# Nearest-code refinement with codes stored as 129-component rows

## The reference

```
x = x + L0(gn(x))   # 3x3 conv -> softmax weights for five dilated 3x3 filters; 1x1 conv; batch norm
x = x + L1(gn(x))   # for each pixel the nearest of 8192 codes (128 components)
x = x + L2(gn(x))   # depthwise 3x3 with kernels from the pooled image
x = x + L3(gn(x))   # two deformable 3x3 convs, each with group norm and relu
```

```
d   = sum(z**2) + sum(codebook**2, axis=1) - 2 * z @ codebook.T
idx = argmin(d, axis=1)
out = codebook[idx]
```

## Time and profile before

| | us |
|---|---|
| median of 3 runs | 1754.48 (1754.34 to 1756.48) |
| profiled execution | 1753.79 |
| its span | 1752.0 |
| PE busy | 1330.8 (76%) |
| DVE busy | 1173.5 (67%) |
| POOL busy | 1039.5 (59%) |
| ACT busy | 413.9 (24%) |

### The profile page before, as it was taken

How to read it: one execution, slowest core, us unless ns; L and a number is a source line. 1 busy time by engine, 2 the same in 40 slices (tenths; PEclk the granted TensorE clock), 3 DMA queues, 4 the chain that set the end, 5 groups by cost and what they waited for, 6 DMA issues and landing times.

```text
span 1752.0 us, 22932 instructions
## 1 busy us (share of the span) xinstructions
PE 1330.8 (76%) x7898; PEld 923.5 (53%) x7898; DVE 1173.5 (67%) x1526; ACT 413.9 (24%) x1280; POOL 1039.5 (59%) x950
## 2 busy tenths in 40 slices
PE   5899999398889987689645468688776877867775
PEld 2455555153344443244345456677666675766675
DVE  4578687689999999988843763654455444564444
ACT  2240000324423332242321122132211221111111
POOL 4268576205444344244477877677777777777772
PEclk9899999699999998899866778898887988878877
DMA  4020000102111111052256579678787887777773
GB/s 148 29 92 1 1 0 0 43 1 55 52 40 43 43 43 49 6 159 84 56 161 180 167 209 278 192 229 247 228 245 210 247 243 235 224 231 211 210 211 117
DMA packets 104985, 228.66 MB, mean 131 GB/s; under 512 B 16740, under 2 KB 54372, under 8 KB 104620
## 3 DMA queue, kind: packets, MB, share of 16 engines
q0 software_dynamic: 59328, 191.30, 37.5%
q1 hardware_dynamic: 45548, 35.97, 6.6%
HBM read 205.15 MB, written 22.07 MB: 130 GB/s over the span
## 4 chain that ended last, share of the span: by engine, by line
POOL 29%; PE 19%; issue 18%; DVE 12%; ACT 1%; DMA 1%; DVEq 0%; POOLq 0%; ACTq 0%
POOL code_region L1745 11%; POOL max_region L1745 6%; POOL late_region L1745 6%; POOL early_region L1745 5%; PE score L1200 4%; PE score L1201 4%; PE score L1202 4%; PE score L1221 3%; DVE max_region L1591 3%; DVE x L266 2%; DVE code_region L1626 2%; PE turn_ps L1230 1%; PE turn_ps L1100 1%; DVE fine L1456 1%; DMA late_region<-in_codes,code 1%
## 5 line engine op out<-in xcount | busy, mean ns | idle before, releaser
L1591 DVE SCALAR_TENSOR_TENSOR max_region<-score,nc,max_region 128x512 f32<-128x512 f32 x504 | 351.3, 738 | 40.1 <-PE score L1202 37.8
L1745 POOL DMA_INDIRECT code_region<-corners,lead_region x261 | 248.5, 952 | 79.5 <-issue 79.2
L1626 DVE TENSOR_TENSOR code_region<-score,code_region 128x4608 f32<-128x4608 f32 x29 | 143.6, 4956 | 137.7 <-DMA code_region<-corners,lead_region 137.4
L1221 PE MATMUL score<-ident,code_region 128*128 128x128 f32 x1044 | 153.2, 319 | 73.4 <-DVE code_region L1626 73.4
L674 POOL TENSOR_TENSOR prod_acc<-prod_acc,prod_pool 128x752 f32<-128x752 f32 (+8 forms) x112 | 149.1, 1331 | 96.2 <-DVE prod_pool L647 88.8
L1221 PEld LDWEIGHTS score<-ident,code_region 128*128 128x128 f32 x1044 | 147.5, 169 | 78.2 <-DVE code_region L1626 78.2
L1393 ACT COPY code_region<-score 128x384 f32<-128x384 f32 x144 | 68.5, 479 | 410.3 <-PE score L1221 410.3
L1745 POOL DMA_INDIRECT max_region<-corners,lead_region x126 | 125.3, 995 | 46.1 <-issue 38.1
L1745 POOL DMA_INDIRECT early_region<-corners,lead_region x135 | 127.7, 946 | 41.0 <-issue 40.8
L1745 POOL DMA_INDIRECT late_region<-corners,lead_region x126 | 127.6, 1012 | 38.9 <-issue 38.1
L1200 PE MATMUL score<-early_region,code_region 128*128 128x512 bf16 x320 | 122.5, 383 | 25.9 <-DVE max_region L1591 19.6
(11 more groups left out here) (197 smaller groups left out, 2674.9 us busy)
## 6 DMA issues: line engine op xcount, KB each, us to landing
corners<-lead_region SPq DMA_DIRECT2D x72, 192.0 KB, 4.6
corners<-lead_region SPq DMA_DIRECT2D x8, 576.0 KB, 6.8
code_region<-corners,lead_region POOLq DMA_INDIRECT x261, 3.7
codes_t<-in_codes_t SPq DMA_DIRECT2D x8, 512.0 KB, 3.7
codes_n<-in_codes SPq DMA_DIRECT2D x8, 512.0 KB, 3.5
x<-in_x SPq DMA_DIRECT2D x2, 1152.0 KB, 6.5
out<-x SPq DMA_DIRECT2D x4, 576.0 KB, 3.2
early_region<-corners,lead_region POOLq DMA_INDIRECT x135, 3.7
```

The lines of the kernel that those rows point to most:

```text
L1221: mm = pe.matmul(tps[g][:, k * P:(k + 1) * P], quads[T % SLOTS][:, 3 * g + k, c * P:(c + 1) * P], ident, start=c == 0, stop=c == CORNERS - ...
L1591: dve.scalar_tensor_tensor(r, score[SLOT[k]][:], nc2[:, m:m + 1], r, ALU.add, ALU.max).then_inc(dve_took, 1)
L1626: dve.tensor_tensor(q4, bc(wps[:, u * n:(u + 1) * n], P), q4, ALU.mult).then_inc(weighted, 1)
L1745: pool.indirect_dma_start(quads[T % SLOTS][:, k, :], None, table[j].rearrange("n s c -> n (s c)"), bass.IndirectOffsetOnAxis(index[j % B][ ...
```

## The change

The half norms are no longer a tensor of their own. `CodeNorms` becomes `CodeRows`: each slot has room for 129 components a code. A group is loaded into components 0 to 127 of its slot, ACT squares it and then writes minus half the sums into component 128, and SP stores the slot in DRAM as `code_rows`, of 1032 numbers for a block of eight codes. SP stores group g - 2 and waits until it has landed before it loads group g. `gather` reads `code_rows`; the multiply's z has a 129th component of 1, set once, so ACT's sum over 129 products is the score. On DVE `subtract` and `select` are gone, and their places in `parts`. POOL multiplies the block's number by 8 behind each gather and adds the place in `fetch`, before the fetch's DMA.

```diff
-class CodeNorms:
+class CodeRows:
...
+        self.cn = tools.sb(ctx, "codes_n", [P, self.SLOTS, PER, ROW])     # ROW = P + 1
...
     def sp(self, sp):
+        def store(g):
+            sp.wait_ge(self.appended, g + 1)
+            sp.dma_start(self.code_rows[g * P:(g + 1) * P, :], self.cn[:, g % self.SLOTS].rearrange("p j c -> p (j c)"))\
+                .then_inc(self.stored, 16)
+
         for g in range(GROUPS):
             s = g % self.SLOTS
             if g >= self.SLOTS:
-                sp.wait_ge(self.squared, PER * (g - self.SLOTS + 1))
-            sp.dma_start(self.cn[:, s, :], self.a["codes"][g * P:(g + 1) * P, :]).then_inc(self.cn_in[s], 16)
-        sp.wait_ge(self.halved, 2)
-        sp.dma_start(self.half_norms.rearrange("(g p) j -> p g j", p=P),
-                     self.c2.rearrange("p (g j) -> p g j", g=GROUPS)).then_inc(self.stored, 16)
-        sp.wait_ge(self.stored, 16)
+                store(g - self.SLOTS)
+                sp.wait_ge(self.stored, 16 * (g - self.SLOTS + 1))
+            rows = self.a["codes"][g * P:(g + 1) * P, :].rearrange("r (j c) -> r j c", c=P)
+            sp.dma_start(self.cn[:, s, :, 0:P], rows).then_inc(self.cn_in[s], 16)
+        for g in range(GROUPS - self.SLOTS, GROUPS):
+            store(g)
+        sp.wait_ge(self.stored, 16 * GROUPS)
...
     def act(self, act):                       # in the loop over g, behind the eight squares
+            act.wait_ge(self.squared, PER * (g + 1))
+            act.mul(self.cn[:, s, :, P], self.c2[:, g * PER:(g + 1) * PER], -0.5).then_inc(self.appended, 1)
...
-        act.mul(self.c2[:], self.c2[:], 0.5).then_inc(self.halved, 1)
...
-                act.copy(zt, z_ps[:]).then_inc(zt_ready, 1)
+                act.copy(zt[:, :, 0:P], z_ps[:]).then_inc(zt_ready, 1)
...
-            def subtract(n, u): ...
-            def select(n, u): ...
             def fine_find(n, u):
-                apart.wait_ge(sel_step, 1 + 4 * (PXT * (n - 1) + u) + 1)
+                apart.wait_ge(summed, PER * (PXT * (n - 1) + u + 1))
...
-                        for i, part in enumerate((subtract, fine_find, fine_place, select))}}
+                        for i, part in enumerate((fine_find, fine_place))}}
...
             def gather(n, u):
-                pool.indirect_dma_start(cand[u % 2], None, a["codes"], off).then_inc(cand_in[u % 2], 16)
-                pool.indirect_dma_start(half[:, u, :], None, half_norms, off).then_inc(cand_in[u % 2], 16)
+                pool.indirect_dma_start(cand[u % 2], None, code_rows, off).then_inc(cand_in[u % 2], 16)
+                pool.tensor_scalar(block_code[:, u:u + 1], block_id[:, u, 0:1], float(PER), None, ALU.mult)\
+                    .then_inc(block_coded, 1)
             def multiply(n, u):
-                v = cand[u % 2].rearrange("p (j c) -> p j c", c=P)
-                zb = zt[:, u, :].unsqueeze(1).to_broadcast([P, PER, P])
+                v = cand[u % 2].rearrange("p (j c) -> p j c", c=ROW)
+                zb = zt[:, u, :].unsqueeze(1).to_broadcast([P, PER, ROW])
                 pool.tensor_tensor(v, v, zb, ALU.mult).then_inc(multiplied, 1)
             def fetch(n, u):
-                apart.wait_ge(sel_step, 1 + 4 * (PXT * c + u + 1))
+                pool.wait_ge(sel_step, 2 * (PXT * c + u + 1))
+                pool.wait_ge(block_coded, PXT * c + u + 1)
+                pool.tensor_tensor(code[:, u:u + 1], block_code[:, u:u + 1], fine_id[:, u, 0:1], ALU.add)\
+                    .then_inc(coded, 1)
+                apart.wait_ge(coded, PXT * c + u + 1)
...
             pool.sem_inc(x_added, 1)
+            pool.memset(zt[:, :, P:ROW], 1.0).then_inc(ones_ready, 1)
+            pool.wait_ge(ones_ready, 1)
             pool.memset(zeros, 0.0).then_inc(zeroed, 1)
```

More of the change, by code:

```diff
@@ L40 @@
 PX = 512
+ROW = P + 1
 NPX = N // PX
@@ L704, in layer0 @@
                    (gb[:], a["gamma_beta"])])
-            ch, cl, nc2, half_norms = codes
+            ch, cl, nc2, code_rows = codes
             with ExitStack() as parts:
@@ L709, in layer0 @@
             with ExitStack() as parts:
-                beside = CodeNorms(nc, tools, parts, a, nc2, half_norms)
+                beside = CodeRows(nc, tools, parts, a, nc2, code_rows)
                 branches(nc, tools, xpad, wta, wtb, sel_a, sel_b, w_scale, y, stats, beside)
@@ L861, in carve, with finale @@
     return out
-def finale(nc, tools, a, half_norms, x, xpad, ident, gm32, gm8, nc2, depthwise, norm, places, out):
+def finale(nc, tools, a, code_rows, x, xpad, ident, gm32, gm8, nc2, depthwise, norm, places, out):
     PXT, STEPS = PX // P, GROUPS // 2
@@ L921, in finale @@
         block_id = tools.sb(ctx, "block_id", [P, PXT, 8], U32)
-        half = tools.sb(ctx, "half", [P, PXT, PER])
+        block_code = tools.sb(ctx, "block_code", [P, PXT], U32)
         fine = tools.sb(ctx, "fine", [P, PXT, PER])
@@ L1279, in sum_products @@
                 for j in range(PER):
[L1280 removed]
+                    v = cand[u % 2][:, j * ROW:(j + 1) * ROW]
                     act.activation(v, v, ACT.Identity, accum_out=fine[:, u, j:j + 1]).then_inc(summed, 1)
@@ L1450, in place_block @@
                 dve.max_index(block_id[:, u, :], best[:, u, :], maxima[(n - 1) % 2][:, u, :]).then_inc(found, 1)
[L1454 to L1456 removed]
             def fine_find(n, u):
[L1459 removed]
+                apart.wait_ge(summed, PER * (PXT * (n - 1) + u + 1))
                 dve.max(fine_best[:, u, :], fine[:, u, :]).then_inc(sel_step, 1)
             def fine_place(n, u):
[L1463 removed]
+                apart.wait_ge(sel_step, 2 * (PXT * (n - 1) + u) + 1)
                 dve.max_index(fine_id[:, u, :], fine_best[:, u, :], fine[:, u, :]).then_inc(sel_step, 1)
[L1466 to L1471 removed]
             def choose(n, u):
[L1474 removed]
                 fine_find(n, u)
                 fine_place(n, u)
[L1477 removed]
             def subtract_z(n):
```

42 lines of the change are left out of this document (15 added, 27 removed).

## The result

| | before | changed |
|---|---|---|
| median of the runs, us | 1755.48 (1753.09 to 1757.47, 6 runs) | 1743.25 (1739.09 to 1747.83, 6 runs) |
| ratio to before | | 0.9928, 95% interval 0.9908 to 0.9948 |
| the profiled execution, and its span, us | 1753.79, 1752.0 | 1742.20, 1740.4 |
| DVE busy in the stretch of the earlier trace rows, us | 488.46 | 475.46 |

The change is 12.2 us faster; 16.6 were forecast, to 1737.9. The time of 1743.25 lies in the range of 1732 to 1748, but outside the likeliest case's own range (1733 to 1741). What happened is, in the main, the forecast in the search together with a small piece of rival A' at the start.

A forecast was written before the change was run, and what follows sets the result against it. DVE was taken to bound the search, PE close behind, and POOL's row gathers the last 816 us; 10.3 + 2.8 + 1.9 + 1.6 = 16.6 us gained, 1753.79 - 16.6 + 0.69 = 1737.9 us, range 1732 to 1748.

The forecast's parts named there:

- the likeliest case: The forecast itself: gains in search and first job, no cost at the start; 1737.9 us, chance 0.56.
- rival A': First stage: store chain partly late, slot cycle 11 to 15 us, PE stands 1 to 14; 1740 to 1751, chance 0.18.
- What bounds, and the search: DVE sets the search's pace, PE close behind; without stalls chunks 1 to 5 take 51.2 us each, gaining 10.3.
- The 20.3 us of blocked DVE: Search: excess time of the two small DVE operations, L1456 and L1470, over some 0.15 us each.
- B: Search: the stall was mostly hidden by PE's backlog and waits with ACT; gain 6.5, 1748 us, chance 0.08.
- C: Search: DVE freed wholly, steps 2 and 3 fall to PE's 11.25 us, chunk 8 gives 3; 1732 us, chance 0.08.
- D: Chunks 6 to 8: the stall moves to the taps or corner weights; gain 12, 1742 us, chance 0.06.
- The rule of the stall: DVE beside POOL: only DVE operations with two SBUF inputs are blocked; no candidate left in chunks 1 to 5.
- Chunks 6 to 8: Search's end: chunk 6 gains 2.8 us, chunk 7 gains 1.9, chunk 8 is taken as 0, up to 3.
- The first job: POOL is the bound: half gathers saved, less additions and semaphore waits, gain 1.6 us; ends -3 and +5.
- The first stage: Code slots: cycle of 3.2 store, 4.0 load, 2.8 squares is 10.0 us; ACT free at 125.8, cost 0.
- the slack of 2.3: First stage: ACT is free 2.3 us before PE asks for its copy of y; beyond that, delays cost.

The follow-up runs named there:

- e10: Kernel before, `subtract` replaced by a MAX8 into an unused buffer and `select` by a one-column copy; 1745.26 us, ratio 0.9945.
- e4: Changed kernel with three code slots, plus an unused two-input DVE subtraction on 8 columns before each `fine_find`; 1739.94 us in a single run.
- e8: Kernel before, its two small two-input DVE operations (`subtract`, `select`) turned into one-input operations of the same size; 1746.41 us, ratio 0.9972.
- e1: Kernel before with only the first stage's store chain added (129-component slots, each group stored and awaited), search unchanged; 1760.11 us, ratio 1.0047.
- e6: Changed kernel with three code slots, plus an unused second gather of 8 numbers a block behind each row gather, awaited; 1741.35 us, ratio 0.9934.
- e3: Changed kernel with three code slots, `select` back on DVE and POOL's two small operations gone; 1739.04 us, ratio 0.9920.
- f1: The changed kernel as it is, measured again against the kernel before, side by side with f2; 1741.38 us, ratio 0.9930.
- f2: Changed kernel with three code slots and, in the first job, POOL's waits filled with row gathers; 1733.92 us, ratio 0.9893.

## Why the prediction was right and where it failed

*What bounds, and the search.* Right. DVE's stalls were on the path: chunks 1 to 5 gave 10.4 for 10.3 (the changed kernel) and 8.3 by lifting the stall alone (e10). (The 20.3 us of blocked DVE add up to 20.2.) All chunks lie between 51.08 and 51.38 where 51 to 51.6 was said. B, that the stall was mostly hidden, is refuted for the stalls of about 2 us that there were, and holds for those up to 1 us (e4): some 0.9 us of each were hidden. C didn't come: steps 2 and 3 take 11.8 and mostly 11.7 us, and PE's waits there are for DVE's units. C was also priced too low: with both steps at PE's 11.25 a chunk would be 50.1, which is 5.5 us in five chunks and not 2.5. D didn't come: the taps took 2747 ns in the mean for 2760 before. They were stalled already, and still are (the longest took 3.9 us, 4.0 before).

*The rule of the stall.* Right for this change, too narrow in itself (e8); that the change happened to put nothing of the kind in place of the two lines was luck as far as the rule goes. Had the change put a multiplication by a scalar in the subtraction's place, the rule would have promised some 10 us in chunks 1 to 5, where e8 shows 3.7.

*Chunks 6 to 8.* Chunk 6 gave 2.9 for 2.8, and e10, with the stall alone gone, gave 3.3. Chunk 7 gave 0.5 for 1.9 and chunk 8 1.7 for 0: together 2.2 for 1.9, which is chance. In chunk 7 the stall was worth 1.2 (step 2: 18.75 to 17.56 us, at 0.91 and 0.90 of the clock), since 0.9 of it had been hidden; the half gathers, put at nothing in the search, were worth 1.0 (step 1: 17.10 to 16.07); and the low clock of the last step took 1.7. Chunk 8 is the clock's. The kernel e1, with both small operations in place and stalls of 2.0 and 1.2 us in chunk 8, takes 135.0 us for the two chunks, the changed one 135.5.

*POOL.* 0.2 us for the small operation was right (214 and 188 ns in the median), so was 0.8 for the semaphore. The first job gave 1.8 for 1.6, but its parts were larger on both sides: the half gathers were worth 2.6 or more (e6) where 2.5 was the sum, and the additions and their waits cost 1.6 to 2.1 (e3) where 0.9 was. About 1 us more came from what no term had; no run tells from what. That POOL's work is hidden in the search is shown by e6 for all chunks but the seventh.

*The first stage: the step that failed.* "So a slot's cycle is 3.2 + 4.0 + 2.8 = 10.0 ... ACT is free at 125.8 ... Cost 0." The structure of the sum was right (one slot's cycle three times, each us on it costs 3); two of its terms were too small, the store above all. Over all groups the store landed in 4.4 us in the median, not 3.2, and the load in 4.5, not 4.0. The two stores that had no load in flight beside them (93.05 and 132.87) landed in 2.6, the six others in 3.9 to 5.6: the other slot's load, which the 3.2 left out, goes with the longer time, though no run takes it away. The 3.2 came from the output's store, and with the same row after at 3.5 it was no firm number either. SP's own issues show the chain of slot 1, whose last load is group 7 (start us, us):

```profile
101.62 0.55 SPq L836 DMA_DIRECT2D codes_n<-in_codes  x1
...
112.78 0.55 SPq L836 DMA_DIRECT2D codes_n<-in_codes  x1
...
125.48 0.55 SPq L836 DMA_DIRECT2D codes_n<-in_codes  x1
```

Between these loads lie 11.2 and 12.7 us, and from the load before them (86.28) to the first it is 15.3, where ACT was still at work on group 0 when the load landed. From the slot's first store to its last (96.30 to 132.87) the three cycles are 36.6 us together and not 30: the three stores took 5.3, 4.4 and 5.6 (15.3 for 9.6), the three loads 4.0, 4.3 and 4.6 (13.0 for 12.0). The last group went out at 125.48 and ACT ended at 133.0; against 125.8 that is 7.2, less the slack of 2.3: 4.9, and PE stood 4.9. All of it was in A' with "cycle 11 to 15", given 0.18. The error was to write a cost of nothing at a slack of 2.3 us, where each us on a store or a load costs 3: an error of 0.8 in the pair was enough, and the landings in the earlier trace rows alone ran from 3.5 to 9.9. The lower clock behind the pause was in no term.

By the formula of the Trainium skill (DMA: Bandwidth & Descriptors, "Anatomy of one DMA") either transfer would take an estimated 3.2 us. The page gives it for a DMA that GpSimd issues, and these are issued by SP, which my prediction didn't say. The rows here are on both sides of it: 2.6 for a store by itself, 3.9 to 5.6 for one beside a load, 4.0 to 5.7 for the loads in pieces of 512 bytes; the measurement decides.

*The sum.* The search and the first job had 16.6 forecast and gave 17.3 (10.4 + 2.9 + 0.5 + 1.7 + 1.8), the closeness of which owes something to the errors in chunks 7 and 8 that cancel; the tail added 0.5; the start and chunk 0 took 6.2 where 0 was forecast. (Chunk 0's 0.4 is scatter: its first step takes 11.3 to 11.8 us over the profiles.) 11.6 is what is left.

## What to carry to other kernels

A short operation that takes a dozen times its neighbour's duration in some instances is the first thing to look for in a list of groups, and order of time names its partner; but ask of the replacement too whether it can be caught, and ask whether the stall is longer than what the engine behind it can absorb: read that from steps that differ in one stall alone. A buffer that is loaded, worked on and stored back in a ring of two adds store and load to each turn; where an engine in order waits behind it, take a third slot unless the slack is several times the error of a landing time multiplied by the turns. Where an engine waits for its own semaphore before a DMA, put independent issues in between.

## What was not expected of the hardware

- DVE beside a POOL multiply: a float32 multiplication by a scalar on 8 columns, one input, took 595 ns in the mean, 2.64 us at worst (e8), as much as one with two inputs; MAX8 and FIND_INDEX8 on the same columns took 0.16 and at most 0.18, and a one-column uint32 copy 0.14.
- It goes the other way too. Beside a tap of chunk 6 (L267, two SBUF inputs, 2.6 us) a POOL multiply of the changed kernel took 3.67 us for its usual 2.19, and the issue of an indirect DMA behind another 3.1 for 0.95.
- The same stall cost nothing up to 1.0 us (e4), and from 1.84 to 2.32 its duration less some 0.9 (e1, e3, e8, the kernel before).
- POOL's multiply became shorter with more columns, 2.19 us for 1032 and 2.35 for 1024 (medians). No run changed the layout alone, so the reason is open.
- PE got 52 matmuls done in 15 us after its pause of 4.9 us, 64 without one; from its first to its second copy of y it then took 1.5 us longer.
- The same step of the search took 14.9 or 16.5 us (chunk 8), 16.3 or 18.0 (chunk 7), with a granted clock of 1.00 or 0.90 to 0.91. In a balance by stretches the granted clock has to stand beside each stretch.
- A store of 516 KB landed in 2.6 us with no load in flight and in 3.9 to 5.6 with one (the changed kernel); in f1 and f2 the first store took 4.5 and 4.6 with none in flight.
